# VectorE's order in gated cross-attention with routed experts, and a new passage between the two stages

## What is computed

```python
x = x + tanh(g_xattn) * attention(layernorm(x), ctx)   # 32 batches of 128 tokens, 16 heads of 64, 128 keys of width 64
x = x + tanh(g_ffn)   * moe(layernorm(x))
# attention: softmax(q k^T / 8) v, all heads joined, @ Wo + bo
# moe: s = sigmoid(x @ gate_w^T); choice = s + bias; 4 groups of 8 experts, a group scored by its two best;
#      the two best groups stay, then the 8 best experts; weights s / sum(s) * 2.5
#      expert e: (silu(x @ wg^T) * (x @ wu^T)) @ wd^T, 32 of width 64, and a shared one of width 128 for every token
```

## Time and profile before

| | us |
|---|---|
| median of 3 runs | 693.19 |
| lowest and highest | 692.09, 695.07 |
| the profiled execution | 695.34 |
| its span | 693.5 |
| PE busy | 662.6 (96%) |
| DVE busy | 504.2 (73%) |
| ACT busy | 369.2 (53%) |
| POOL busy | 285.8 (41%) |

### The profile page before, as it was taken

The page is one execution under the profiler, slowest core; times in us unless marked ns, Lnnn a source line. Parts: engine busy times, 40 slices in busy tenths (PEclk is TensorE's granted clock), DMA queues, the critical chain, the costliest instruction groups (busy, mean ns, idle before and its releaser), DMA issues. The chain is left out here.

```text
span 693.5 us, 13643 instructions
## 1 busy us (share of the span) xinstructions
PE 662.6 (96%) x3676; PEld 477.5 (69%) x3676; DVE 504.2 (73%) x1329; ACT 369.2 (53%) x691; POOL 285.8 (41%) x317
## 2 busy tenths in 40 slices
PE   8998999999999999999899899999999999999997
PEld 6555666666556666666556778878787888888785
DVE  5877876766757577685866886969687786869565
ACT  4363454554545555555465445555555555565553
POOL 4213131332323222232320555656565665756564
PEclk9998999999999999999999999999999999999999
DMA  7322222323223222332223825555353636464550
GB/s 192 80 61 72 58 71 64 89 60 76 59 76 80 69 77 60 76 88 62 54 58 94 186 62 127 135 113 138 81 136 86 160 80 153 107 149 114 124 139 15
DMA packets 63244, 65.58 MB, mean 95 GB/s; under 512 B 26080, under 2 KB 41568, under 8 KB 63200
## 3 DMA queue, kind: packets, MB, share of 16 engines
q1 hardware_dynamic: 63200, 65.07, 38.5%
HBM read 61.64 MB, written 2.88 MB: 93 GB/s over the span
## 5 line engine op out<-in xcount | busy, mean ns | idle before, releaser
L494 POOL TENSOR_TENSOR halves<-area,halves 128x512 fp32r<-128x512 f32 x135 | 175.2, 1298 | 147.8 <-ACT halves L620 142.7
L633 ACT ACTIVATE area<-bank 128x512 f32<-128x512 f32 x136 | 81.4, 599 | 113.8 <-PE bank L1112 112.9
L574 ACT ACTIVATE area<-bank 128x512 f32<-128x512 f32 x128 | 69.5, 594 | 129.8 <-PE bank L1175 129.8
L1068 DVE TENSOR_TENSOR bank<-area,bank 128x512 f32<-128x512 f32 x128 | 88.7, 693 | 54.9 <-PE bank L1112 54.6
L1186 PE MATMUL bank<-area,ctx_keys 128*65 128x512 f32 (+1 forms) x256 | 127.4, 611 | 0.8 <-ACT u_odd L528 0.8
L1110 PE MATMUL bank<-x2t_hi,w_hi 128*128 128x512 f32 x272 | 110.8, 407 | 1.6 <-DVE area L1078 1.6
L762 DVE TENSOR_REDUCE row_max<-bank 128x4 f32<-128x512 f32 x128 | 81.9, 682 | 35.0 <-PE bank L1146 32.5
L440 POOL TENSOR_TENSOR ctx_hi<-ctx_raw,ones_col 128x128 fp32r<-128x128 f32 x32 | 18.0, 562 | 216.4 <-DMA ctx_raw<-ctx_t 216.4
L1111 PE MATMUL bank<-x2t_hi,w_lo 128*128 128x512 f32 x272 | 107.1, 394 | 0.0
L1112 PE MATMUL bank<-x2t_lo,w_hi 128*128 128x512 f32 x272 | 106.4, 391 | 0.0
L620 ACT ACTIVATE halves<-area 128x512 fp32r<-128x512 f32 x136 | 85.0, 626 | 18.9 <-DVE area L1078 18.6
(11 more groups left out here) (129 smaller groups left out, 1106.5 us busy)
## 6 DMA issues: line engine op xcount, KB each, us to landing
wbc<-rows_dram SPq DMA_DIRECT2D x128, 256.0 KB, 4.3
inverse_bc<-inverse_dram SPq DMA_DIRECT2D x64, 256.0 KB, 3.9
w_raw<-experts SPq DMA_DIRECT2D x32, 102.0 KB, 2.0
ctx_raw<-ctx_t SPq DMA_DIRECT2D x32, 64.0 KB, 1.9
ctx_keys<-ctx_nat SPq DMA_DIRECT2D x32, 64.0 KB, 2.1
out<-area SPq DMA_DIRECT2D x7, 256.0 KB, 4.0
max_rows<-max_t SPq DMA_DIRECT2D x64, 4.0 KB
area<-wq_t SPq DMA_DIRECT2D x1, 512.0 KB, 4.5
```

The costliest lines, as they stand in the source:

```text
L494: nc.gpsimd.tensor_tensor(hid_lo[:, u % SLOTS, :], hid[:, u % HIDS, :], raw(hid_hi[:, u % SLOTS, :]), ALU.subtract).then_inc(hidlo_ready, 1)
L574: nc.scalar.activation(probs_t[:, k, :, :], st_ps[q][:].rearrange("p (h n) -> p h n", h=4), ACT.Exp)\
L633: nc.scalar.activation(silu_g[:, u % 2, :], gate_ps[u % 2][:], ACT.Silu).then_inc(silu_ready, 1)
L1068: nc.vector.tensor_tensor(up_ps[u % UPS][:], silu_g[:, u % 2, :], up_ps[u % UPS][:], ALU.mult)\
```

## The change

On DVE, in the attention: `chunk_stats(1)` stands ahead of chunk 0; the other calls of `chunk_stats` stand one step sooner and ahead of the `normalise` or `g_low` of their step, where they stood behind; the Newton levels of chunk 1 stand in two steps and not three; `g_low` stands ahead of `residual`, `batch_mean` and `keep_means`. In chunk 7 the routing levels stand later by one to four levels. On PE and ACT the first transposition (`transpose_norm(8)`, `x2t_out(0)`) stands half a batch later. For chunk 0 alone the low sigmoid is exp(x) / (1 + exp(x)), with one more DVE instruction; ACT makes it behind both `u_out` of its batch. Batch 30 is scaled right behind the attention, ahead of the experts' first unit, and batch 31 at units 4 and 5; their projections stand at units 2 and 7. SP stores and spreads the inverses of batch 31 between the loads of the weights' groups 0 and 1, and 1 and 2. Nothing that is computed is left out.

```diff
-LN_AT = {0: range(0, 5), 1: range(5, 9), 2: range(9, RSTD_LEVELS)}
+LN_AT = {0: range(0, 8), 1: range(8, RSTD_LEVELS)}
-STATS_AT = {3: (2,), 4: (3,), 5: (4,), 6: (5, 6), 7: (7,)}
+STATS_AT = {2: (2,), 3: (3,), 4: (4,), 5: (5,), 6: (6, 7)}
-SEAM = {4: (1, 7), 5: (7, 13), 6: (13, 16), 7: (16, 21)}
-LATE = {NB - 2: 5, NB - 1: 11}
-NORM_AT = {(2, 1): ((NB - 2, 0), (NB - 2, 1)), (6, 1): ((NB - 1, 0),), (7, 1): ((NB - 1, 1),)}
+SEAM = {4: (1, 4), 5: (4, 9), 6: (9, 15), 7: (15, 21)}
+LATE = {NB - 2: 3, NB - 1: 8}
+NORM_AT = {(4, 1): ((NB - 1, 0),), (5, 1): ((NB - 1, 1),)}
...
             store_rows(0)
-            for g in range(WBC_SLOTS):
+            load_group(0, 0)
+            store_inverse(NB - 1, (NB - 1) % 2)
+            load_group(0, 1)
+            spread_inverse(NB - 1, (NB - 1) % 2)
+            for g in range(2, WBC_SLOTS):
                 load_group(0, g)
-            store_inverse(NB - 1, (NB - 1) % 2)
-            spread_inverse(NB - 1, (NB - 1) % 2)
...
-                nc.scalar.activation(silu_low, ps[:, CB * NE:2 * CB * NE], ACT.Silu).then_inc(sig_ready, 1)
+                nc.scalar.activation(silu_low, ps[:, CB * NE:2 * CB * NE], ACT.Silu if c > 0 else ACT.Exp)\
+                    .then_inc(sig_ready, 1)
...
                     exp_of(t, 1, 1)
                     if last and b == 1:
                         sigmoid_high(0, ut_ps)
-                        sigmoid_low(0, ut_ps)
                     u_out(t, b % 2, 0, 0)
...
                     u_out(t, b % 2, 0, 1)
+                    if last and b == 0:
+                        x2t_out(0, ut_ps)
+                    if last and b == 1:
+                        sigmoid_low(0, ut_ps)
...
             def sigmoid_high(c):
                 dve.wait_ge(sig_ready, 2 * c + 2)
+                if c == 0:
+                    step(nc.vector.tensor_scalar(quarter(1), silu_low, 1.0, None, ALU.add))
+                    so_far(c)
                 step(nc.vector.reciprocal(quarter(1), quarter(1)))
...
             dve.wait_ge(const_ready, 6)
+            chunk_stats(1)
...
                                 normalise(t - 2, b % 2, 1)
+                        if step_of_chunk == 2 and first:
+                            ln_apply(1, CB)
+                        if first:
+                            for n in STATS_AT.get(step_of_chunk, ()):
+                                chunk_stats(n)
+                        if h == 1 and b % 2 == 1 and not last:
+                            g_low(2 * c + 2 + b // 2, b // 2)
+                        if h == 1:
                             if not (first and b < 3):
                                 residual(t - 3)
...
             residual(NB - 3)
+            normalise(NB - 2, (NB - 2) % 2, 0)
+            invert(NB - 1, (NB - 1) % 2)
+            normalise(NB - 2, (NB - 2) % 2, 1)
...
-                if first and (u, place) == (0, 1):
-                    invert(NB - 1, (NB - 1) % 2)
...
-                    if b == (0 if last else 1):
+                    if b == 1 and not last:
                         transpose_norm(c + 1, ut_ps)
...
                     weigh(t, b, 0, 0, c + 1)
+                    if last and b == 0:
+                        transpose_norm(c + 1, ut_ps)
```

More of the change, by code:

```diff
@@ L261, in free_of, with steps_before @@
             return UNITS * c - UNITS + before + 1
+        def steps_before(c):
+            return ROUTE_STEPS * c + (1 if c > 0 else 0)
         block = stack.enter_context(nc.Block())
@@ L589, in attention @@
                         x2t_out(1, scores_ps[1])
-                    if last and b == 0:
-                        x2t_out(0, ut_ps)
                     if not last and b == 1:
@@ L966, in attention @@
                                 take_max(t + 2, b % 2, h, q)
-                        if h == 0:
-                            if not first:
-                                batch_stats(t - CB, b)
-                        else:
+                        if h == 0 and not first:
+                            batch_stats(t - CB, b)
+                        if h == 1:
                             if not (first and b == 0):
@@ L1001, in attention @@
                             normalise(t - 2, b % 2, 0)
-                        if h == 1 and b % 2 == 1 and not last:
-                            g_low(2 * c + 2 + b // 2, b // 2)
                         if step_of_chunk == 2 and not last:
```

22 lines of the change are left out of this document (7 added, 15 removed).

## The result

The changed kernel takes 670.97 us (median of 4 runs, 669.68 to 671.43) beside 693.62 for the kernel before (4 runs, 692.09 to 695.07): a ratio of 0.9671, with a 95% interval of 0.9645 to 0.9697. That is 22.65 us less. The forecast was 674.0 with a range of 669 to 684. The profiled execution took 671.43 with a span of 669.6, where that of before took 695.34 and 693.5.

A forecast was written before the change was run, and what follows sets the result against it. PE was taken as the bound throughout, so only its waits and their clock falls could go: 3.4 + 6.0 + 3.4 + 3.5 + 5.1 = 21.4 us off 695.34 gives 673.9, forecast 674.0, range 669 to 684.

The forecast's parts named there:

- Chunk 0: First attention chunk: earlier statistics and Newton levels take 3.4 us (1.5 to 5.1) from PE's four waits of 5.07 us.
- The loop: Chunk loop of the attention: g_low ahead of residual removes 6.0 of 6.6 us of PE's waits, bounds 0 and 6.6.
- Chunk 7: Last attention chunk: of 4.72 us idle, 0.3 stays and a new wait of 1.0 (0 to 2.0) comes; 3.4 won.
- The passage: First units of the experts: PE's waits of 1.99 and 1.58 us go, 3.5 of 3.57 won; at worst 1.6 stays.
- The port rule: DVE and GpSimd share SBUF ports: batch 31's two normalise lose 0.5 us each, the sum up to 1.0 lower.
- The clock: PE's clock over the kernel: three of four falls of 1.7 us go with PE's waits, 5.1 won, bounds 0 and 6.8.
- The falls stay: Rival: the clock's falls come on their own, so 5.1 us stay and the time is 679; chance 0.13.
- One stage gives nothing: Rival: a stage's waits end by something other than DVE's order; 3.4 to 6.0 us less won, 681 to 684; chance 0.15.
- most is given back: Rival: in loop and chunk 0 another engine is as late as DVE; only 8.6 us won, 687; chance 0.07.
- Slower: Rival: residual behind g_low holds PE's transpose_max, 2.47 us paid 14 times, 34.6 in all, 708 us; chance 0.03.
- signs of being wrong: Removed PE waits reappearing with a DMA or ACT as releaser, or the clock falling as often as before.

The follow-up runs named there:

- single parts: The kernel before with one part of the change each: g_low ahead of residual 685.18 us, chunk 0's order 686.96, new passage 683.95, first transposition half a batch later 688.62.
- third group: Runs on one chip beside the kernel before (692.58 us): waits filled 692.51, Exp alone 689.77, changed kernel again 670.27, the same with routing levels where they stood before 668.88.
- filled to measure: The kernel before with 2, 3 and 2 unread products in PE's waits of 1.79, 2.22 and 1.99 us: 692.51 us beside 692.58, ratio 0.999.

## Why the prediction was right, step by step

- **Chunk 0, 3.4 (1.5 to 5.1): 2.9.** The mechanism is as told, but for what stands below on `g_project`. The second wait fell to 0.38, as put (0.3 to 0.4). The third went to 1.38 and not 1.1; `g_project` starts at 60.63, 1.5 later than the 59.1 forecast and so outside the 1 us that the prediction allowed it, of which 0.84 is the start of the kernel (7.46 us of warm-up products in place of 6.62) and 0.39 the inverses' way (7.55 in place of 7.16). The start is no work of the change: it takes 6.04 to 7.56 in the 14 profiles. The first and the last wait went whole, as told: 5.07 became 1.76, 3.3 won for 3.5. The step that failed is `chunk_stats(1)` ahead of the chunk, which I let cost nothing if DVE idles there, with no row on it. DVE does idle, 1.06 behind these statistics, and still its next `take_max` comes 0.28 later against PE; the profile names no releaser for it ("issue"), and what it waits for is open. What the prediction did not see is that PE's own pace did not count ahead of this `g_project`: in the kernel before and in the four others with its chunk 0 (`g_low`, passage, transposition, Exp), `g_project` starts at 64.04, 64.11, 63.78, 63.75 and 63.94, although the warm-up took 6.62, 7.50, 7.16, 7.36 and 6.37, and only the first has a fall ahead of it. DVE's `normalise` behind the inverses, at 58.97 to 59.33 in all five, and the statistics behind it set that time. In the seven kernels with the new order `g_project` starts at 58.87 to 60.79, which is the length of the warm-up and 52.8 to 53.3 more: there PE's start does count.
- **The loop, 6.0: the waits for `g_low` fell from 6.6 to 0.6**, and the idle time by 6.7. `residual` behind it held nobody, as the 1.13 of PE's work between scores and transposition had said. This is the best sized term; alone in the kernel before it gave 7.3, without any gain of the clock. In the changed kernel's second profile 1.5 us of these waits are left, in six of at most 0.3.
- **Chunk 7, 3.4: 2.7.** The waits of 1.92 and 1.11 went. The new wait ahead of the transposed weights is 0.97 for 1.0 forecast. What I had not seen is that the waits for `u_odd`, with ACT as releaser, would grow from 0.53 to 0.91. They sum to 0 and 0.4 in the two profiles with the old routing levels, 0.5 in the changed kernel's second, 0 with Silu, and the first of them alone is 1.33 and 1.37 in two of the single parts. So they vary a lot, also between two executions of one kernel, and no cause is shown. The gain was put on the wrong edit in part: moving the levels later is not needed once Exp stands there, and the wait of 1.0 for the weights stands in both profiles of the changed kernel and in neither with the old levels; whether the time shows it is open (above).
- **The passage, 3.5 of 3.57: all 3.57 went**, with the two `normalise` at 1.20 and 1.22 in place of 3.44 for the pair.
- **The port rule, up to 1.0 more for batch 31: not in this profile** (1.20 and 1.22), but in the second of the old routing levels (2.29 and 1.22; in the first 1.21 and 1.22). Its price depends on 0.1 us of which engine starts first. It is a part of the spread between runs and no fixed term.
- **The clock, 5.1: wrong in number and in price, and nearly right in sum by the profiled pair.** I took three of four falls at 1.7. All four went in the profiled execution. In the typical run at most 2.3 fall to at most 0.2 (mean clock 0.9942 and 0.9995 in the third group), 3.7 us of lost clock, at 0.73 each 2.7 us. Two steps failed. One profiled execution was read as if it were typical for the clock; the correction of one fall between it and the median was too small. And each fall was put at 1.7, also the one between the waits of 1.79 and 2.22, which cost no time of its own: `g_project` starts as late without it, after a wait of 3.5 to 4.0 in place of 2.22. In the sum for the profiled pair that does no harm, since the idle term took only 1.1 of the wait that the fall had shortened; as a price for a typical run, which doesn't have this fall, it is wrong.
- **The sum.** In the profiled pair: 2.9 + 6.7 + 2.7 + 3.6 of idle time and 6.8 of clock are 22.7, of 23.9 measured. PE's busy time fell by 8.5 over the four stages, 1.7 more than the falls. I can't place that 1.7; the start of the kernel took 0.84 the other way. For the medians, 15.9 + 2.7 are 18.6 of 22.65. Of the 4.0 that remain, 0.2 to 1.4 may be idle time: the two long waits of chunk 0 are 4.01 together in the profile of before and 4.18 to 5.40 in the four others with its chunk 0, where no fall stands between them. The other 2.6 to 3.8 stay open. The waits were forecast at 16.3 and gave 15.9 in the pair, the clock at 5.1 and gave 6.8 in the pair but about 2.7 in the median. What the runs account for, 18.6 to 20.0, would be 673.6 to 675.0; that the median is lower still, 3.0 below the forecast, is not explained.
- **The rivals.** "The falls stay" fell: they went with the waits, both by the change and by filling (`g_low` alone took no lost clock away). "One stage gives nothing" and "most is given back" fell with the four single parts, each of which is faster than before with an interval that excludes 1. "Slower" fell with `g_low` alone.
- **The prediction's own arithmetic.** "Slower, 708" is 674 + 34.6, with the 21.4 still won; 34.6 in place of them would be 730. And the lower end, 669 "(no fall, no new wait)", needs more than these two, which give 674 - 1.7 - 1.0 = 671.3; the upper bounds of chunk 0 and of the loop (1.7 and 0.6 more) bring it to 669. Of the signs of being wrong, two did appear in a small form: ACT as a releaser, in waits that were there before (0.54 and 0.37 now), and a DMA behind the 1.38 that is left in chunk 0.

## What to carry to other kernels

Where one engine is the bound and idles in short waits, read for each wait which instruction of the late engine stood ahead of the one that was waited for, and move that one behind it. Alone, these moves gave 28.0 where all together gave 22.65: each gain is real, their sum is too high. Before you price what an engine loses ahead of one of its waits, see whether the end of that wait moves with it from run to run; in chunk 0 it didn't, and the loss cost nothing. Price a fall of the clock from many runs, not from the one that was profiled, and don't count it where a longer wait stands behind it. When an edit makes another one needless (Exp took away what the later routing levels were for), try the kernel without the second.

## What the runs showed of the hardware

- The clock fell from 2.4 to 1.2 GHz, beside waits of 1.8 to 2.3 us: at 2.30 here with Silu, and at the earlier trace rows next to 1.79 and 1.99. The fall of the loop, from 203.6 on, has only 0.93 and 0.32 close ahead of it (at 201.25 and 202.23), and the one from 368.9 on in the kernel with the later transposition 1.33 and 0.38. With the waits of 1.79, 2.22 and 1.99 filled the mean granted clock rose from 0.9942 to 0.9987, with no other change. No wait has its fall for certain: the same 1.92 ahead of the transposition had none in the profiles of before, of the passage and of Exp alone, and one in those of the kernel with chunk 0's order (PEclk 0.72 from 329 to 333) and of the one filled to measure (0.77 from 333 to 337), where all is alike at this place. I had argued from the first alone that it has none. The Trainium skill (TensorE: Matmul & The Clock Gate, section "HAM oscillation — how this bites in real kernels") ties falls to longer gaps than these; by the filled kernel, shorter ones matter too.
- PEclk doesn't tell all of PE's speed. The records of the first warm-up products start some 0.85 us apart and then 0.43, while PEclk reads 1.00 in each of these microseconds. The changed kernel's profile has two more of the slow ones than that of before, hence 7.46 us in place of 6.62; the length varies from 6.04 to 7.56 in the 14 profiles.
- An ACT_TABLE_LOAD took 1.28 us, and the next activation started 0.02 behind its end, twice in a row. The Trainium skill (ScalarE: Activation LUTs, section "What ACT_TABLE_LOAD costs") puts 2.66 us on a switch, with a drain; no drain stands in these rows.
- From SP's store of the weights' rows to its load of them it took 1.9 us in one profile and 3.7 in another, and 1.7 to 2.1 in eleven of the other twelve. With PE's waits below 1 us such a difference decides which wait is seen, and it is as large as what the last experiments tried to tell apart.
